# Moving raw x and LoRA-A loads in the hand-planned issue order of a fused LoRA and adapter kernel

## What is computed

```python
def layer0(x, weight, bias, lora_a, lora_b, scaling, adapter_id):
    base = jnp.einsum('bsi,oi->bso', x, weight) + bias
    low = jnp.einsum('bsi,bri->bsr', x, lora_a[adapter_id])
    delta = jnp.einsum('bsr,bor->bso', low, lora_b[adapter_id])
    return base + scaling[adapter_id][:, None, None] * delta

x = x + layer0(x, L0_weight, bias, lora_a, lora_b, scaling, itok_B_1_7)
x = x + jnp.einsum('bij,bkj->bik', x, L1_weight[itok_B_1_14])
```

## Time and profile before

| | |
|---|---|
| median of three runs | 2757.71 us (2757.48 to 2758.25) |
| the profiled execution | 2758.53 us, of which 2756.4 us are the span of the trace |
| PE busy | 2702.5 us (98%) |
| DVE busy | 1777.4 us (64%) |
| ACT busy | 1329.1 us (48%) |
| POOL busy | 708.0 us (26%) |
| DMA | 640.00 MB, 232 GB/s over the span |
| mean granted TensorE clock | 0.992 |

### The profile page before, as it was taken

How to read it: one execution, slowest core, us unless ns; L and a number is a source line. 1 busy time by engine, 2 the same in 40 slices (tenths; PEclk the granted TensorE clock), 3 DMA queues, 4 the chain that set the end, 5 groups by cost and what they waited for, 6 DMA issues and landing times.

```text
span 2756.4 us, 35556 instructions
## 1 busy us (share of the span) xinstructions
PE 2702.5 (98%) x12823; PEld 2234.8 (81%) x12823; DVE 1777.4 (64%) x1582; ACT 1329.1 (48%) x1398; POOL 708.0 (26%) x582
## 2 busy tenths in 40 slices
PE   8799999999899999999989999999999999999999
PEld 6688888888788888888878888888887888888887
DVE  5556776866555657686645565768674656676865
ACT  3333355756433335576633333666663424366665
POOL 4335721412412102141241211114133121012502
PEclk9899999999999999999999999999999999999999
DMA  7958957687455435678736544899984555499996
GB/s 246 347 187 300 347 167 222 221 285 242 155 200 174 154 130 190 207 242 276 236 133 213 183 146 145 287 308 325 388 309 167 191 170 164 147 307 311 312 323 230
DMA packets 193359, 640.00 MB, mean 232 GB/s; under 512 B 22528, under 2 KB 30880, under 8 KB 193184
## 3 DMA queue, kind: packets, MB, share of 16 engines
q1 hardware_dynamic: 192896, 637.20, 68.1%
q10 hardware_dynamic: 288, 0.52, 0.1%
HBM read 646.03 MB, written 58.72 MB: 256 GB/s over the span
## 4 chain that ended last, share of the span: by engine, by line
PE 90%; issue 3%; DMA 2%; DVE 2%; POOL 2%; SPq 1%; ACT 0%; POOLq 0%; ACTq 0%; DVEq 0%
PE acc L942 16%; PE acc L941 16%; PE acc L943 16%; PE acc L888 13%; PE acc L889 13%; PE acc L898 13%; POOL raw L579 1%; PE acc L859 1%; DMA raw<-w 1%; DVE ws L820 1%; PE acc L910 1%; DVE ops L820 1%; DMA raw<-xt 1%; DMA raw<-w_sums 1%; SPq L498 1%
## 5 line engine op out<-in xcount | busy, mean ns | idle before, releaser
L698 ACT CAST ws<-raw 128x1024 fp32r<-128x1024 f32 (+1 forms) x1056 | 1083.2, 1051 | 1129.3 <-PE acc L943 476.5
L820 DVE TENSOR_TENSOR ws<-raw,ws 128x1024 fp32r<-128x1024 f32 (+1 forms) x1024 | 1327.2, 1320 | 458.2 <-ACT ws L698 453.7
L942 PE MATMUL acc<-ws,ops 128*128 128x512 f32 (+1 forms) x2048 | 796.8, 389 | 0.0
L941 PE MATMUL acc<-ws,ops 128*128 128x512 f32 (+1 forms) x2048 | 796.8, 389 | 0.0
L943 PE MATMUL acc<-ws,ops 128*128 128x512 f32 (+1 forms) x2048 | 796.7, 389 | 0.0
L888 PE MATMUL acc<-ops,ws 128*128 128x512 f32 x1792 | 708.3, 395 | 42.1 <-DVE ws L820 38.7
L889 PE MATMUL acc<-ops,ws 128*128 128x512 f32 x1792 | 704.7, 393 | 0.0
L898 PE MATMUL acc<-ops,ws 128*128 128x512 f32 x1792 | 703.3, 392 | 0.0
L604 POOL TENSOR_TENSOR raw<-raw,eye_s 128x128 f32<-128x128 f32 x384 | 341.7, 920 | 1176.5 <-DMA raw<-w 1176.4
L941 PEld LDWEIGHTS acc<-ws,ops 128*128 128x128 f32 x2048 | 384.5, 188 | 80.1
L943 PEld LDWEIGHTS acc<-ws,ops 128*128 128x128 f32 x2048 | 384.4, 188 | 79.6
(11 more groups left out here) (58 smaller groups left out, 534.4 us busy)
## 6 DMA issues: line engine op xcount, KB each, us to landing
raw<-w SPq DMA_DIRECT2D x928, 512.0 KB
raw<-w_sums SPq DMA_DIRECT2D x104, 512.0 KB
raw<-xt SPq DMA_DIRECT2D x96, 512.0 KB
out<-ost SPq DMA_DIRECT2D x128, 256.0 KB, 7.0
cb<-xt SPq DMA_DIRECT2D x60, 512.0 KB, 6.4
w_sums<-raw SPq DMA_DIRECT2D x32, 512.0 KB, 5.1
ost<-a SPq DMA_DIRECT2D x64, 128.0 KB, 2.2
x_sums<-raw SPq DMA_DIRECT2D x16, 512.0 KB, 3.8
```

Source lines behind the costliest of these rows:

```text
L698: ins = eng.copy(hi, src)
L820: ins = eng.tensor_tensor(lo, src, hi, ALU.subtract)
L941: eng.matmul(acc, yh, wh, start=begin, stop=False)
L942: eng.matmul(acc, yh, wl, start=False, stop=False)
```

## The change

The loop that places the extras now compares an extra's key with the key of the split that owned the ring slot last, not with that of the split to be loaded. In group 0 the keys of the extras are also set anew: those of x tiles 2 and 3; the LoRA-A load j = 1 is cut in two parts (`sets`); and the second load of x tile 1 comes after the third block of k = 2. The block ("LA", 0, 3) moves from before k = 2 to before k = 3. In groups 1 to 3 the keys and blocks stay.

```diff
             if k == 2:
-                blocks += [("LA", g, 1), ("LA", g, 3)]
+                blocks.append(("LA", g, 1))
+            if k == (2 if g else 3):
+                blocks.append(("LA", g, 3))
...
-            extra += [(splits_key["X", 0, i % 2 + 1, b] - 0.1, ("x", 0, i, b, 0)) for i in (2, 3) for b in range(G)]
-        extra.append((la_key, ("la", g, 0)))
-        extra.append((te[at["LA", g, 2]] + 0.6, ("la", g, 1)))
-        extra += [(te[at["W", g, 1, 2]] + 4.0 * b, ("x", g, 1, b, 1)) for b in range(G)]
+            extra += [((-1.0, 8.0, 13.0, 14.5)[b], ("x", 0, 2, b, 0)) for b in range(G)]
+            extra += [(splits_key["X", 0, 2, b] - 10.0, ("x", 0, 3, b, 0)) for b in range(G)]
+        extra.append((la_key, ("la", g, 0, (0, 1))))
+        if g:
+            extra.append((te[at["LA", g, 2]] + 0.6, ("la", g, 1, (0, 1))))
+        else:
+            extra += [(te[at["LA", g, 2]] + 0.6, ("la", g, 1, (0,))), (te[at["W", g, 2, 0]], ("la", g, 1, (1,)))]
+        extra += [(te[at["W", g, 1 if g else 2, 2]] + 4.0 * b, ("x", g, 1, b, 1)) for b in range(G)]
     extra.sort()
     split_of = {}
     for n, (key_, _, kind, index) in enumerate(splits):
-        while extra and extra[0][0] <= key_:
-            split_of[len(place)] = (-1, 0, extra.pop(0)[1])
-            place.append(None)
-            prior.append(None)
-            landed.append(0)
         raws[n] = []
         for what in raws_of(kind, index):
+            m = owner[ring % NRAW]
+            begin = splits[split_of[m][0]][0] if m is not None else key_
+            while extra and extra[0][0] <= begin:
+                split_of[len(place)] = (-1, 0, extra.pop(0)[1])
+                place.append(None)
+                prior.append(None)
+                landed.append(0)
             r = len(place)
+            split_of[r] = (n, len(raws[n]), what)
...
-                    for h in range(2):
+                    for h in sets:
```

More of the change, by code:

```diff
@@ L257, in program @@
             pool_no[n, step] = pool_total
-    for n in raws:
-        for i, (r, what) in enumerate(raws[n]):
-            split_of[r] = (n, i, what)
     dadd_no = {number["W", 0, 1, o]: o + 1 for o in range(HT)}
@@ L482, in _ @@
                 if what[0] == "la":
-                    _, g, j = what
+                    _, g, j, sets = what
                     if j:
```

## The result

The changed kernel takes 2719.64 us (median of 4 runs, 2717.23 to 2721.25) against 2757.98 (2757.48 to 2758.49): a ratio of 0.986, with a 95% interval of 0.9843 to 0.9877. The forecast was 2716, with a range of 2704 to 2733. The profiled execution took 2719.66 us with a span of 2717.5, 38.9 us less than that of before. From L261 of the old file on, lines stand six further down in the new one: L888 is now L894, L820 is L826, L859 is L865, L498 is L504, L448 is L454.

What follows compares the result with a forecast made beforehand. TensorE bounds the kernel, busy 2702.5 of 2756.4 us, so only its pauses can be won. 2758.5 - 29.7 (boundaries) - 12.4 (group 0) = 2716.4, less 0.8 for the median: 2715.6, say 2716; range 2704 to 2733.

Steps and rivals of the forecast that it cites:

- Boundaries: Starts of groups 1 to 3: 36.6 us lost today shrink to 2.3 per group, a gain of 29.7 us.
- turns: Group starts: GpSimd and VectorE alternate whole operations; W(g,0,2) ready at 722.1, TensorE 1.8 us idle.
- a mere slowdown: Group starts: GpSimd and VectorE only slow each other; W(g,0,2) ready at 721.6, 1.3 us late.
- Group 0, the middle: Group 0, k = 1: W(0,1,1)'s tiles requested earlier; of 21.2 us lost, 0.5 allowed to remain.
- the walk: Ring supply in group 0, k = 1: W(0,1,5) ready about 96, W(0,1,6) 103, W(0,1,7) 109 us.
- Moving ("LA", 0, 3): Group 0: putting this block in front of W(0,3,0) costs nothing, the same 1.8 us of matmuls.
- Group 0, the start: New stall at W(0,0,5) from X(0,1,1)'s later raw tile: 5.2 us idle plus 3.1 of clock, 8.3 us.
- (a): Group 0: no new stall at W(0,0,5), 2708 us; chance 0.12.
- (b): Group 0: supply of k = 1 keeps its pace, 7.13 us a block; gain 1.1, 2727 us; chance 0.13.
- (c): Groups 1 to 3: a second block held at each boundary, 5.3 us more each; 2732 us; chance 0.12.
- (d): S phases: 36 x loads moved into later slices cost TensorE up to 49 us; 2765 us; chance 0.05.
- (e): Whole kernel: nothing moves, waits reappear behind the later LoRA loads; 2757 us; chance 0.04.

Runs made afterwards that it cites:

- the run with this part alone: Kernel before with only the new placement rule, from group 1 on; keys, blocks and order of group 0 unchanged: 2727.48 us.
- the run with the later key: Changed kernel with the key of X(g,1,0) 6 us later in groups 1 to 3, so it comes behind W(g,0,3): 2712.36 us.
- the run with the later save: Changed kernel with the save of X(0,1,0) nine places behind its load instead of five: 2710.51 us.
- both edits: Changed kernel with X(0,1,0) saved nine places behind its load and the key of X(g,1,0) 6 us later in groups 1 to 3: 2703.89 us.
- LoRA-A loads before the save: Changed kernel with la_key 13.0 instead of 14.0 in group 0, so SyncE issues the LoRA-A loads before the save of X(0,1,0): 2713.49 us.
- fillers: Changed kernel with 30 more matmuls, result unused, in front of W(0,0,5): 2718.19 us.
- again: The changed kernel repeated unaltered, on the same chip as other follow-up runs: 2719.76 us.

## Why the prediction held, point by point

**Boundaries.** Right in mechanism and size. Expected were 2.3 us lost per group in place of 12.2 on average, the profile has 1.9 at the pause and 0.1 later. Measured between GpSimd's starts (709.47, 1391.26 and 2074.28 before, 700.67, 1371.71 and 2042.76 now) and the end, the three groups are 10.8, 12.0 and 7.4 us shorter, 30.1 together, where 29.7 was forecast; the run with this part alone gained 28.7. That the remaining pause is VectorE behind GpSimd was argued in the prediction and is shown by the run with the later key. The dates cannot tell turns from a mere slowdown: W(1,0,2) is ready 12.4 us after GpSimd's start, where turns gave 12.6 and a slowdown 12.1. The lengths can. GpSimd's two operations on X(1,1,1), each by itself:

```profile
706.32 2.40 POOL L585 TENSOR_TENSOR raw<-raw,cb 128x1024 f32<-128x1024 f32 x1
...
708.80 3.25 POOL L585 TENSOR_TENSOR raw<-raw,cb 128x1024 f32<-128x1024 f32 x1
```

The first took its usual 2.4 us although VectorE's split had begun at 706.65; the split ended 1.1 us after it, at 709.81. Then GpSimd's second was the longer one, and VectorE's second split ended 1.1 us after that, at 713.13. This fits the Trainium skill's rule in "SBUF — State Buffer" (Who interferes with whom), that the loser waits for the whole instruction.

**Group 0, the middle.** Right: the 21.2 us lost there fell to 1.5, with 0.5 allowed. The dates of the walk were early. I had W(0,1,1)'s tiles requested from about 49; the first went at 53 and the others from 60.4, because GpSimd was done with X(0,1,3) at 60.0 and not near 54. W(0,1,7)'s tiles were there at 107.45, not near 103, its low half was ready at 114.2, and its block started at 114.4; I had 109 and 111.2. It held because TensorE and the supply slipped together: the late tile of X(0,1,1) delays both. VectorE's sums for W(0,1,1) and W(0,1,7), before and after, give the supply's pace:

```profile
75.94 1.22 DVE L758 TENSOR_TENSOR raw<-raw 128x1024 f32<-128x1024 f32 x1 [15.38 <-POOL raw L589]
...
118.11 1.23 DVE L758 TENSOR_TENSOR raw<-raw 128x1024 f32<-128x1024 f32 x1 [1.66 <-POOL raw L589]
```

```profile
71.23 1.22 DVE L764 TENSOR_TENSOR raw<-raw 128x1024 f32<-128x1024 f32 x1
...
110.50 1.23 DVE L764 TENSOR_TENSOR raw<-raw 128x1024 f32<-128x1024 f32 x1 [1.69 <-POOL raw L595]
```

That is 7.0 us per block before and 6.5 after, both slower than the 5.44 us of matmuls. So the supply keeps up by its lead, not by its pace: W(0,1,1) was ready at 74.8, 5.6 us ahead of its block, and W(0,1,7) only 0.2 us ahead. My volume was half a tile short (four LoRA-A loads of 128 KB are one tile, and four left the stretch, not two): 16.8 MB, 316 GB/s. The DMA engines were full from 75 to 100, at up to 415 GB/s: a mean hid that the traffic bunches, and the Trainium skill's limit near 358 GB/s ("DMA: Bandwidth & Descriptors", Where 436 GB/s comes from) is passed here.

**Moving ("LA", 0, 3).** I gave it nothing as a step and counted its relief inside the stretch. The run without it is 4 to 5 us slower, and its sums for W(0,1,1) and W(0,1,7) are 6.9 us per block apart. So the relief was about half of what group 0 nets.

**Group 0, the start.** The mechanism was right and its size too small by 1.8 us, half of the 3.6 between forecast and result. I took 8.3 us, the profile shows 10.1. The pause is 8.2 us, not 5.2: X(0,1,1)'s tile went out at 36.00, not at 32.6. I carried over only the 5.84 us in which the LoRA-A loads are issued. SP also reads the adapter numbers into registers first, 28.62 - 27.04 = 1.6 us which before lay ahead of 17.49; the save left 0.8 us later, and the eight loads took 6.68 us. That makes 3.2 of the 3.4 us. The clock cost less than I took, 1.9 instead of 3.1. The bound of 9.3 for the term was passed.

**The sum.** 30.1 + 8.8 = 38.9 us, the difference of the two spans. I had 29.7 + 12.4. Group 0 is 3.6 us short: 1.8 at its start, 1.0 in the middle, and 0.7 behind that, where the small pause at 122.47 stood in no term of mine. The boundaries gave 0.4 more. I had also taken 0.8 us off for the median; this time it equals the profiled execution. Together that is the step from 2715.6 to 2719.6.

**Rivals.** (a) is excluded by the profile; the run with the later save shows that 9 us were indeed there to be had. (b) did not come about, but half of its premise holds: the supply's pace rose only from 7.0 to 6.5 us per block. Its price was wrong because it let W(0,1,1) start without a lead. (c) is excluded by the boundary run. (d): no pause stands in an S phase, in any of the eight experiments or in the changed kernel. (e) is excluded.

## What to carry to other kernels

In a queue that issues in order, place each item by when its resource becomes free, not by when the next item is due; a blocking item in front of free slots costs its wait once for every load behind it. When something is moved, list what it passes that can block, saves and stores as well, and carry along all that it issues, register reads too. After each pause that is removed, look at what supplies the same block next: at the boundaries it was VectorE beside GpSimd, for 1.9 us each.

## What the runs showed of the hardware

- A transfer of 512 KB that was requested within 1.8 us of a save and two other tiles took 7.2 us from request to use (28.99 to 36.21), against 4.7 (36.00 to 40.68) in the changed kernel, behind one other tile and the LoRA-A loads.
- What the clock costs behind a pause does not follow its length. Over the two blocks behind W(0,0,5)'s pause, beyond 10.88 us of matmuls: 0.2 us after 2.29 (both edits), 1.8 after 2.73 (LoRA-A loads before the save), 1.9 after 2.32 (fillers), 1.9 after 8.20 (changed kernel), 1.6 after 9.01 (again), 2.8 after 9.70 (X(g,1,0) behind W(g,0,3)). In the slow stretch matmuls start 0.43 us apart, at a granted clock of 0.50 (1.2 GHz). After the pauses of 1.72 us at the boundaries only the first was slower (0.50).
- The stretch of 90 to 95 us moved 415 GB/s between memory and the core.
